# Routers with the gate weights stationary, an expert bias added by VectorE, scatters without a hold between them, and a result stored in four parts

## The reference, cut to what matters

```python
# layer 4, "L1_ffn": 8 experts (4 of width 256, 4 of width 512), every expert computed for every token
logits = xf @ router_w.T                       # 2048 x 8
topw, sel = top_k(sigmoid(logits), 2)          # weights normalised to sum 1 -> combine (2048 x 8)
h = square(relu(einsum('td,edw->tew', xf, W1e)))
out = einsum('ted,te->td', einsum('tew,ewd->ted', h, W2e), combine)

# layer 8, "L3_ffn": attention and layer norm, then 8 experts with a capacity of 256 tokens each
gates = softmax(xf @ wg); idx = argmax(gates)  # one expert a token
slot = idx * cap + loc, if loc < cap           # loc: how many earlier tokens chose the same expert
disp = zeros.at[slot].set(xf, mode='drop')     # rows sent to their expert
h = disp @ w1 + b1;  y = h @ w2 + b2           # per expert: 256 x 256 -> 256 x 1024 -> 256 x 256
out = where(keep, gate_val * y[slot], 0)
y2 = layer_norm(y1 + out);  x = x + y2         # the kernel's result
```

## Time and profile before

| what | us |
|---|---|
| median of 3 runs (lowest, highest) | 2725.27 (2724.52, 2727.11) |
| the profiled execution | 2728.62 |
| its span, from the first to the last instruction | 2726.7 |
| mean granted TensorE clock | 0.955 |
| busy: TensorE, VectorE, ScalarE, GpSimd | 2361.6 (87%), 1294.5 (47%), 995.9 (37%), 128.2 (5%) |

### The profile page before, as it was taken

The page is one execution under the profiler, slowest core; times in us unless marked ns, Lnnn a source line. Parts: engine busy times, 40 slices in busy tenths (PEclk is TensorE's granted clock), DMA queues, the critical chain, the costliest instruction groups (busy, mean ns, idle before and its releaser), DMA issues. The chain is left out here.

```text
span 2726.7 us, 38491 instructions
## 1 busy us (share of the span) xinstructions
PE 2361.6 (87%) x15045; PEld 1680.3 (62%) x15045; DVE 1294.5 (47%) x2609; ACT 995.9 (37%) x2834; POOL 128.2 (5%) x206
## 2 busy tenths in 40 slices
PE   6778887999988999989999999969988897874984
PEld 4455555666655666666666666547876675654773
DVE  6456665777764334333455445654443443231003
ACT  3245564777762111112333333433223442231122
POOL 0000000000000000000000000030010000002003
PEclk8979999999998999999999999999999999796996
DMA  3000001000002000020000000000011000021332
GB/s 113 16 1 1 1 1 40 13 25 13 24 1 93 1 0 1 1 109 8 9 9 9 8 9 1 1 28 0 1 43 40 20 5 16 1 72 61 124 113 66
DMA packets 52534, 74.81 MB, mean 27 GB/s; under 512 B 8050, under 2 KB 41348, under 8 KB 51204
## 3 DMA queue, kind: packets, MB, share of 16 engines
q1 hardware_dynamic: 50820, 68.14, 7.4%
q0 software_dynamic: 1536, 4.20, 0.5%
HBM read 63.94 MB, written 8.39 MB: 27 GB/s over the span
## 5 line engine op out<-in xcount | busy, mean ns | idle before, releaser
L862 ACT ACTIVATE ca_prob<-bank,ca_nmax 128x512 f32<-128x512 f32 x256 | 174.0, 690 | 92.9 <-DVE ca_nmax L929 92.9
L929 DVE TENSOR_REDUCE ca_nmax<-bank 128x1 f32<-128x512 f32 x256 | 164.0, 682 | 56.2 <-PE bank L720 56.1
L862 ACT ACTIVATE na_prob<-bank,na_nmax 128x257 f32<-128x257 f32 x256 | 118.0, 474 | 191.0 <-DVE na_nmax L929 191.0
L1458 PE MATMUL bank<-XN,rf_W 128*128 128x512 f32 x384 | 172.9, 601 | 0.0
L1469 PE MATMUL bank<-rf_W,rf_h 128*128 128x256 f32 x768 | 170.8, 379 | 0.0
L1469 PEld LDWEIGHTS bank<-rf_W,rf_h 128*128 128x128 f32 x768 | 145.9, 190 | 33.1 <-issue 14.8
L734 PEld LDWEIGHTS bank<-cst,ca_prob 128*128 128x128 f32 x1024 | 112.3, 142 | 73.6 <-issue 63.2
L862 ACT ACTIVATE ra_prob<-bank,ra_nmax 128x256 f32<-128x256 f32 x256 | 118.2, 482 | 104.1 <-DVE ra_nmax L929 104.1
L1513 ACT ACTIVATE rf_r<-bank 128x512 f32<-128x512 f32 x96 | 57.4, 598 | 256.3 <-PE bank L1458 256.3
L734 PE MATMUL bank<-cst,ca_prob 128*128 128x128 f32 x1024 | 140.5, 279 | 6.6 <-DVE ca_pT L935 5.9
L929 DVE TENSOR_REDUCE na_nmax<-bank 128x1 f32<-128x257 f32 x256 | 90.8, 417 | 91.5 <-PE bank L720 91.5
(11 more groups left out here) (395 smaller groups left out, 4423.8 us busy)
## 6 DMA issues: line engine op xcount, KB each, us to landing
xl_w<-in_L_ffn_w SPq DMA_DIRECT2D x16, 1024.0 KB
dp_cx<-in_ctx_tok SPq DMA_DIRECT2D x4, 1024.0 KB, 14.1
ca_v<-in_ctx_values SPq DMA_DIRECT2D x8, 512.0 KB, 4.6
rf_W<-in_L_ffn_w SPq DMA_DIRECT2D x8, 512.0 KB, 8.6
na_Wkv<-in_L_xattn_Wkv SPq DMA_DIRECT2D x1, 4096.0 KB
na_cxT<-in_ctx SPq DMA_DIRECT2D x8, 512.0 KB, 3.4
ma_cxT<-in_ctx SPq DMA_DIRECT2D x8, 512.0 KB, 3.3
X<-in_x SPq DMA_DIRECT2D x1, 2048.0 KB, 7.9
```

What stands on the lines that cost most here:

```text
L862: e = act.activation(prob[:, n % 2, u, hh * keys:(hh + 1) * keys], S[u][:, hh * keys:(hh + 1) * keys], ACT.Exp, bias=nmax[:, n % 2, u, hh: ...
L929: v.tensor_reduce(nmax[:, n % 2, u], S[u][:, 0:W].rearrange("p (h k) -> p h k", h=per), AX.X, ALU.max, negate=True).then_inc(maxed, 1)
L1458: mm = pe.matmul(g.bank[n % 3][:], W1[:, k, c * P:(c + 1) * P], g.XN[:, k, gi * GT:(gi + 1) * GT], start=(k == 0), stop=(k == KD - 1))
```

## The change

1. Both routers hold the gate weights stationary. They are padded with zeros to 32 columns (a memset on GpSimd, for which SP waits before the weight's load), and XN moves past them, 512 tokens at a time. The four groups go to four sets of 32 partitions of one PSUM bank: 8 matmuls for all 2048 tokens. ScalarE copies the bank to `lgT`, and four transposes bring the logits back to tokens on partitions.
2. In the routed layer this is done once, at the start; the three later routings and their exponentials go. In the expert layer the four transposes stand behind the second pair of row transposes, and ScalarE's exponential moves behind the fifth copy of rows.
3. The expert bias b2 is loaded to all 128 partitions (128 KB instead of 1 KB), the bias matmuls go, and VectorE adds b2 as it takes the output out of PSUM.
4. SP waits for VectorE (`yc`) before it issues the loads, where it waited for TensorE (`yp`).
5. GpSimd waits once for all copies of rows and issues the 16 scatters with no hold between them.
6. The result is stored in the last layer norm, 512 tokens at a time, each part behind its own addition; `end_layer` now comes behind the stores.

```diff
@@ layer_norm_phase
+                if store is not None:
+                    stored = g.sem(f"{tag}_stored")
+                    for gi in range(NG):
+                        sp.wait_ge(added, KD * (gi + 1))
+                        sp.dma_start(part(feature_rows(store), gi), part(dst, gi)).then_inc(stored, 16)
+                    sp.wait_ge(stored, 16 * NG)
@@ routed_ffn_layer
         def prefetch(sp):
-            sp.dma_start(Wr[:], feature_rows(A["L1_ffn_router_w"])).then_inc(router, 16)
+            sp.wait_ge(blank, 1)
+            sp.dma_start(Wr[:, :, 0:E], feature_rows(A["L1_ffn_router_w"])).then_inc(router, 16)
...
-                def route(gi):
-                    if gi >= 2:
-                        pe.wait_ge(added, KD * (gi - 1))
-                    elif gi == 1:
-                        pe.wait_ge(taken, 1)
-                    for t in range(4):
-                        for k in range(KD):
-                            mm = pe.matmul(BR[:, t * E:(t + 1) * E], g.XN[:, k, gi * GT + t * P:gi * GT + (t + 1) * P],
-                                           Wr[:, k], start=(k == 0), stop=(k == KD - 1))
+                def route():
+                    for k in range(KD):
+                        for gi in range(NG):
+                            mm = pe.matmul(g.bank[4][32 * gi:32 * gi + 32, :], Wr[:, k], g.XN[:, k, gi * GT:(gi + 1) * GT],
+                                           start=(k == 0), stop=(k == KD - 1), skip_group_check=True)
                     mm.then_inc(logits, 1)
+                def turn_logits():
+                    pe.wait_ge(laid, 1)
+                    for j in range(4):
+                        mm = pe.transpose(BR[:, j * P:(j + 1) * P], lgT[:, j * P:(j + 1) * P], ident)
+                    mm.then_inc(lg_turned, 1)
...
                 pe.wait_ge(router, 16)
-                route(0)
+                route()
                 hidden(0)
+                turn_logits()
                 for i in range(NI):
...
-                    if e == 3 and gi + 1 < NG:
-                        route(gi + 1)
@@ expert_layer
-                                 (b2[:, e % 2], A["L3_ffn_b2"][e:e + 1, :])):
+                                 (b2[:, e % 2], A["L3_ffn_b2"][e, :].unsqueeze(0).to_broadcast([P, D]))):
...
                     for e in range(E):
+                        sp.wait_ge(yc, 2 * e + 2)
                         if e + 2 < E:
-                            sp.wait_ge(yp, 2 * e + 2)
                             load_weights(sp, e + 2)
                             load_rows(sp, e + 2)
-                        sp.wait_ge(yc, 2 * e + 2)
...
+                    po.wait_ge(row_copied, TT // 2)
+                    hold_pool(g, po).then_inc(held, 1)
                     for t in range(TT):
-                        po.wait_ge(row_copied, t // 2 + 1)
-                        hold_pool(g, po).then_inc(held, 1)
                         po.indirect_dma_start(sent, bass.IndirectOffsetOnAxis(ap=slot[:, t:t + 1], axis=0), rows[:, t], None)\
                           .then_inc(sent_all, 16)
-                        po.wait_ge(held, t + 1)
...
-                            pe.matmul(g.bank[5 + t][:, 0:D], g.c("ones")[0:1, :], b2[:, e % 2], start=True, stop=False)
...
-                        if q == 2:
+                        if q == 5:
                             act.wait_ge(st, 3)
                             act.activation(pe8[:], dif[:], ACT.Exp).then_inc(eg, 1)
...
-                            v.tensor_copy(yt[:, e % 2, t], g.bank[5 + t][:, 0:D]).then_inc(yc, 1)
+                            v.tensor_tensor(yt[:, e % 2, t], g.bank[5 + t][:, 0:D], b2[:, e % 2], ALU.add).then_inc(yc, 1)
```

More of the change, by code:

```diff
@@ L144, in build @@
         if STAGES >= 8:
-            position_attention_layer(g)
+            position_attention_layer(g, out)
             end_layer()
-        store_phase(g, out)
 def hold_pool(g, po):
@@ L208, in layer_norm_phase @@
     with nc.Block() as block:
-        if prefetch is not None:
+        if prefetch is not None or store is not None:
             @block.sync
             def _(sp):
-                prefetch(sp)
+                if prefetch is not None:
+                    prefetch(sp)
+                if store is not None:
[4 more added lines that the diff above has]
+                    sp.wait_ge(stored, 16 * NG)
         if prepare is not None or resid is not None:
@@ L1396, in routed_ffn_layer @@
         W2 = sb("W2", [P, CH, D])
[L1397 to L1398 removed]
+        Wr = sb("Wr", [P, KD, 32])
+        lgT = sb("lgT", [P, GT])
+        ex = sb("ex", [P, 4 * NG, E])
         pr = sb("pr", [P, 4, E])
@@ L1513, in rectify @@
                         act.activation(r[:, n % 3], g.bank[n % 3][:], ACT.Relu).then_inc(relu, 1)
-                take(0)
+                act.wait_ge(logits, 1)
+                act.activation(lgT[:], g.bank[4][:], ACT.Copy).then_inc(laid, 1)
                 rectify(0)
-                for i in range(NI):
-                    if i + 1 < NI:
-                        rectify(i + 1)
-                    gi, e = divmod(i, E)
-                    if e == 3 and gi + 1 < NG:
-                        take(gi + 1)
+                take()
+                for i in range(1, NI):
+                    rectify(i)
             @block.vector
@@ L2078, in position_attention_layer, with expert_layer @@
                              project(Wo, KD), finish, wl, 7, mask=mask, own_keys=True)
-        expert_layer(g, lambda prefetch, prepare: layer_norm_phase(g, "npa", src=Y, dst=g.XN, gain=gain, shift=shift,
+        expert_layer(g, out, lambda prefetch, prepare: layer_norm_phase(g, "npa", src=Y, dst=g.XN, gain=gain, shift=shift,
                                                                    prefetch=prefetch, prepare=prepare))
-def expert_layer(g, norm):
+def expert_layer(g, out, norm):
     nc, A = g.nc, g.A
@@ L2125, in expert_layer @@
             gs = sb("gs", [P, 2, 2, D])
-            wl, made, zeroed, zs, held, sent_all = (g.sem("xl_" + n) for n in (
-                "weights", "made", "zero_made", "zeroed", "held", "rows_sent"))
+            wl, made, zeroed, zs, held, sent_all, blank = (g.sem("xl_" + n) for n in (
+                "weights", "made", "zero_made", "zeroed", "held", "rows_sent", "gate_blank"))
             ldw = [g.sem(f"xe_weights{j}") for j in range(2)]
@@ L2205, in _ @@
                     pe.wait_ge(wl, 48)
-                    for t in range(TT):
-                        for k in range(KD):
-                            mm = pe.matmul(g.bank[0][:, t * E:(t + 1) * E], g.XN[:, k, t * P:(t + 1) * P], Wg[:, k],
-                                           start=(k == 0), stop=(k == KD - 1))
+                    for k in range(KD):
+                        for gi in range(NG):
+                            mm = pe.matmul(g.bank[0][32 * gi:32 * gi + 32, :], Wg[:, k], g.XN[:, k, gi * GT:(gi + 1) * GT],
+                                           start=(k == 0), stop=(k == KD - 1), skip_group_check=True)
                     mm.then_inc(lp, 1)
                     for q in range(TT // 2):
+                        if q == 2:
+                            pe.wait_ge(laid, 1)
+                            for j in range(4):
+                                mm = pe.transpose(g.bank[3][:, j * P:(j + 1) * P], lgT[:, j * P:(j + 1) * P], ident)
+                            mm.then_inc(lg_turned, 1)
                         if q >= 4:
@@ L2372, in _ @@
                     v.wait_ge(merged, TT // 2)
-        layer_norm_phase(g, "nxl", src=g.XN, dst=g.X, gain=gain, shift=shift, resid=g.X)
+        layer_norm_phase(g, "nxl", src=g.XN, dst=g.X, gain=gain, shift=shift, resid=g.X, store=out)
 HOST_T = ("L1_xattn_w_qkv", "L1_xattn_w_proj", "L1_ffn_router_w", "L3_xattn_W_src", "L3_xattn_W_tgt", "L3_xattn_W_out",
```

67 lines of the change are left out of this document (34 added, 33 removed).

## The result

The changed kernel takes 2701.55 us (median of 4 runs, 2690.65 to 2707.10), the kernel before 2726.19 beside it (4 runs, 2724.52 to 2728.26). The ratio is 0.9907, 95% interval 0.9887 to 0.9927: faster by 0.9%, some 25 us. The profiled execution took 2699.22 us with a span of 2697.4, 29.3 less than the 2726.7 before, at a mean granted clock of 0.958 where it was 0.955.

The account below looks back on a forecast made before the run. It took TensorE to bound the routed layer, and chains and a DMA loop the expert layer. Terms -4.6 - 9.0 - 1.7 - 0.2 - 3.7 = -19.2 us took the median 2725.3 to 2706.1, range 2698 to 2714.

Parts of the forecast that it names:

- Routed layer: Routed layer: three later routings go, the first becomes 16 overlapping records plus four transposes; -4.6 us, +2.5 without overlap.
- The expert layer's routing: Expert layer, norm to slots: logits matmuls fall from 13.65 to 4.04 us, VectorE still waiting for counting matmuls; -9.0 us.
- Scatters: GpSimd's sixteen scatters in the expert layer: spacing falls from 1.38 to 1.25 to 1.28 us; -1.7 us.
- store: End of the kernel: time behind the last addition falls from 8.4 to 4.7 us; -3.7 us.
- Experts: Expert loop: -4.7 us at equal clock and +4.5 for clock; -0.2 us, between -2.6 and +5.6.
- The bias matmul: Expert loop: sixteen bias matmuls of 0.63 us each leave TensorE; -10.1 us.
- The clock: Expert loop: longer waits slow the second products by 2.1 us each, 12.6 in all against 8.1; +4.5 us.
- Rival (a): Expert loop: longer waits lower the clock more, a long slow stretch behind every wait; +5.8 us, 2712; chance 0.15.
- (d): Expert loop runs better than at present: waits fall, clock holds, routing gains a further 1 us; 2699; chance 0.07.
- The two delays: Expert loop, six waits: loads issued 0.5 us later and bias queued ahead of the input, 0.4 us; +5.4 us.
- (b): Both routings: the router matmuls do not overlap; +7.1 and +9.6 us, 2723; chance 0.05.
- (c): Expert loop: broadcast bias holds up the experts' input and the kernel gets slower; 2736 at 5 us each; chance 0.03.

Follow-up runs that it names:

- experiment 1: The changed kernel run once more with no edit, for a second trace: 2696.48 us, ratio 0.9892 to the kernel before.
- experiment 5: The changed kernel with the two loops of both routings swapped, so records of one column set follow each other: 2687.29 us (one run).
- Experiment 9: Kernel with rows early and bias late, plus ScalarE's exponential table loaded ahead and the exponential two copies earlier: 2669.68 us, ratio 0.9790.
- experiment 8: The kernel before with one edit, the next but one expert's input loaded ahead of the weights: 2701.71 us, ratio 0.9920.
- experiments 3: The changed kernel with input loaded ahead of the weights, broadcast bias behind the input, weights issued when TensorE is done: 2671.04 us, ratio 0.9798.
- experiment 6: The kernel before, run once more with no edit for a second trace: 2730.12 us (one run).
- experiment 7: The changed kernel with six unread matmuls of 256 columns ahead of each of the six waits: 2688.38 us, ratio 0.9870.
- experiment 4: The changed kernel with the bias matmuls back and b2 in one partition, SP still waiting for VectorE: 2709.35 us, ratio 0.9940.

## Why the forecast held, and what it had wrong

The forecast was faster, with the sum of -19.2 us giving 2706.1; the median fell by 24.6 us to 2701.55, and in the repetition by 28.4 to 2696.48. The first is inside the range of 2698 to 2714, the second is 1.5 us below it. The profiled execution fell by 29.4, to 2699.2, where the sum gave 2709.4. With single runs 16 to 19 us apart, a median inside the range is in part luck; the stages say more.

**Routed layer** (-4.6; -6.6). The three later routings went, 5.67 us, as computed. The overlap of the router matmuls was right, and experiments 1 and 5 show it at both clocks. The transposes cost 0.15 us less than 0.59, and the 16 records 0.5 less than by the row of 256 columns. The latter comes from the earlier trace rows, whose row is the second half of one of 32 records: all 32 start at 813.83 and take 1.87 us, 0.94 for sixteen and not 1.01. The remainder is the clock: it is whole again after 5.3 us (the window from 850.10 to 853.60 has 0.75, half of it at either level) where it had taken 8.6, and experiment 1 shows that this varies from one execution to the next.

**The expert layer's routing** (-9.0; -10.0). Right, and in the place named: the matmuls went from 13.65 to 3.6 us. What was wrong is the link that is late next. I wrote that VectorE must wait for the counting matmuls; it waits for the exponential, whose place I had taken for free. The clock had recovered ahead of the last transposes, so TensorE was done sooner. Experiment 9 shows that with the exponential out of the way 1.4 us more lie there.

**Scatters** (-1.7; -1.6) and **store** (-3.7; -4.6, of which 4.0 behind the last addition) were right; the parts landed in 2.7 to 3.2 us, where the sum had 3.0. The prediction's estimate of 3.2 us comes out near too, but the Trainium skill (DMA: Bandwidth & Descriptors, Anatomy of one DMA — SWDGE (gpsimd) path) gives its figure for transfers that GpSimd issues, and SP issued these.

**Experts** (-0.2; -8.4). This is the step that failed, in two terms of its sum.
The bias matmul: I took 0.63 us from the starts of two rows in a timeline and -10.1 in all; experiment 8 against 3 has 0.78 and -12.5.
The clock: I had it at 12.6 us of slow products instead of 8.1, +4.5, because the waits grow. The waits did grow, 1.03 each for 0.9 forecast, but the products' loss was 5.8, and the loop's "rest" fell by 2.1. So of the 8.2 us by which the loop beat its forecast the clock is 6.6 and the bias matmuls are 2.4, and the longer waits take 0.8 back.

What length does can be counted over the seven profiles with six waits each. The loss is the time from the transposes to the next expert's first product, beyond the same stretch at full clock:

| wait | how many | followed by a loss | of 1.6 to 1.7 us | of 2.7 to 3.3 us |
|---|---|---|---|---|
| 1.67 to 2.46 us | 21 | 13 | 13 | 0 |
| 2.92 to 4.09 us | 21 | 11 | 6 | 5 |

Longer waits did not lower the clock more often, but the dear losses stand behind them alone, and not behind each: the wait of 3.10 us in the earlier trace rows cost 3.3, one of 3.19 in experiment 6 cost 1.6, and one of 3.25 in experiment 5 nothing. Kernels with bias matmuls lost behind 14 of 18 waits, those without behind 10 of 24. That the removed matmuls themselves made the clock fall less often would explain the sign of my error; it was not tested, and 42 waits are few. What holds is the cruder rule: an idle TensorE may lose its clock (experiment 7), and with no waits there is no such loss (experiments 3 and 8). Rival (a), a long slow stretch behind every wait, did not come. The time of (d) came nearest to the two medians, and for the larger part by its clock, which held behind three waits of six; but the waits, which were to fall for it, rose.

The two delays came out near their sum with the shares reversed: the broadcast costs 0.66 us (experiment 4) and not 0.4, the later issue, by 0.46 us, the remaining 0.37 and not 0.5.

**Rivals** (b), no overlap, and (c), a broadcast that holds the input up by 3 us or more, did not come.

**What was not asked.** The change left the loop's own limit where it was: 256 KB of input queued behind 2 MB of weights. Taking this away is worth 22.8 us in the kernel before and, together with the bias behind the input, 26.9 in the changed one (loop alone), about as much as all six edits, and it takes the clock's share with it.

## What to carry to other kernels

- Where a loop is closed through a DMA queue, look first at what stands ahead of the transfer that the engine waits for. A small input asked for one step earlier, ahead of the big one, removed waits and clock loss together, and one moved line was worth nearly as much as six edits.
- Price a removed instruction by the period of the loop with and without it if you can find both, since the distance between two starts in a timeline leaves out part of what it displaces (0.63 against 0.78 to 0.82 us).
- Do not fit a slope to one event of the clock. Say that idle time puts it at risk and what each slow product costs, and leave its sign in the range.

## What the runs showed of the hardware

- Matmuls with 32-column weights, written to four sets of columns, overlap also at 512 columns and in both orders tried: 16 records in 1.92 to 1.95 us at clock 1.00 and 3.64 to 3.67 at 0.50, where one 128-column record takes 0.85 at half clock.
- A broadcast of 1 KB to 128 partitions, ahead of a small load in a queue that is busy with 2 MB, delays it by 0.66 us (experiment 4 against the changed kernel).
- Six matmuls of 256 columns in place of idling kept the clock through a 3 us wait: products of 7.07 us instead of up to 9.56. The Trainium skill (TensorE: Matmul & The Clock Gate, HAM oscillation — how this bites in real kernels) tells of a loop that waits for a DMA in every pass and starts every pass cold; here that held behind 3 of 6 waits in one execution of the changed kernel, so as a rule for each pass the trace does not bear it out.
- Behind 42 waits of TensorE for a DMA, of 1.67 to 4.09 us, the clock fell in 24 cases. A fall cost 1.6 to 1.7 us, and 2.7 to 3.3 in 5 of the 11 behind waits of 2.9 us and more.
- The clock alone moved one untouched stage between 168.1 and 175.6 us, and the routed layer of one kernel between 361.9 and 366.0.
